# A gated graph network and graph attention on 128 graphs: the attention probabilities turned by one transposing DMA a group in place of four TensorE transposes, and the gather's second half in a bank of its own

## What is computed

```python
# layer 0: three rounds of message passing with a GRU cell
h = relu(layernorm(x))
for i in range(3):
    m = h @ weight[i]
    aggr = A^T @ m                    # A = (adj != 0), per graph
    h = gru_cell(aggr, h, w_ih, w_hh, b_ih, b_hh)
x = x + h
# layer 1: graph attention
h  = relu(layernorm(x))
Wh = h @ W.T
s1, s2 = Wh @ a1, Wh @ a2
e   = leaky_relu(s1[:, None] + s2[None, :], 0.2)
att = softmax(where(adj == 0, -inf, e))
x = x + att @ Wh
```

## Time and profile before

| | |
|---|---|
| time, median of 3 runs | 1867.82 us (1867.44 to 1868.47) |
| the profiled execution | 1866.37 us, of which 1864.6 us are its span |
| TensorE busy | 1797.0 us, 96% |
| VectorE, ScalarE, GpSimd busy | 1420.2 (76%), 1028.3 (55%), 346.5 (19%) us |
| granted TensorE clock, mean | 0.993 |
| DMA queue of the transfers | 26.7% of 16 engines |

### The profile page before, as it was taken

The page is one execution under the profiler, slowest core; times in us unless marked ns, Lnnn a source line. Parts: engine busy times, 40 slices in busy tenths (PEclk is TensorE's granted clock), DMA queues, the critical chain, the costliest instruction groups (busy, mean ns, idle before and its releaser), DMA issues.

```text
span 1864.6 us, 32405 instructions
## 1 busy us (share of the span) xinstructions
PE 1797.0 (96%) x10620; PEld 958.6 (51%) x10620; DVE 1420.2 (76%) x2801; ACT 1028.3 (55%) x1822; POOL 346.5 (19%) x778
## 2 busy tenths in 40 slices
PE   6999999999999999999999999999999999999995
PEld 5444555545555455555545555454554545555453
DVE  6667787777877877877777877777877777877776
ACT  5555555555555546555555556555555555555543
POOL 1022030311303122030310303113031220303101
PEclk9999999999999999999999999999999999999998
DMA  3323232322313223222222313223222322323111
GB/s 103 73 63 69 52 77 48 87 59 56 87 36 90 51 52 88 56 73 51 73 68 51 93 31 101 45 56 90 56 74 45 77 70 51 73 51 84 29 47 51
DMA packets 292000, 120.50 MB, mean 65 GB/s; under 512 B 207489, under 2 KB 291969, under 8 KB 291969
## 3 DMA queue, kind: packets, MB, share of 16 engines
q1 hardware_dynamic: 291968, 120.11, 26.7%
HBM read 52.96 MB, written 16.78 MB: 37 GB/s over the span
## 4 chain that ended last, share of the span: by engine, by line
issue 58%; POOL 13%; DVE 9%; PE 8%; ACT 7%; DMA 3%; POOLq 1%; ACTq 0%; DVEq 0%; SPq 0%
DMA ht_s<-h_s 3%; PE z_bank L318 3%; PE r_bank L318 2%; POOL ln_gnn L310 2%; DVE n_pre L887 2%; POOL ln_att L310 2%; ACT relu_gnn L270 2%; DVE dot_terms L933 1%; PE hn_bank L318 1%; ACT tanh_r L819 1%; PE in_bank L318 1%; ACT relu_att L270 1%; DVE stats_att L248 1%; ACT u_hi L845 1%; POOL ln_att L306 1%
## 5 line engine op out<-in xcount | busy, mean ns | idle before, releaser
L824 ACT ACTIVATE n_out<-n_pre,bih 128x512 f32<-128x512 f32 x192 | 137.9, 718 | 255.0 <-DVE n_pre L887 252.8
L318 PE MATMUL hn_bank<-ht_s,wh_hi 128*128 128x512 f16 x768 | 228.4, 379 | 1.7 <-PEq L426 1.7
L318 PE MATMUL r_bank<-ht_s,wh_hi 128*128 128x512 f16 x768 | 228.4, 379 | 0.0
L318 PE MATMUL z_bank<-ht_s,wh_hi 128*128 128x512 f16 x768 | 228.4, 379 | 0.0
L882 DVE SCALAR_TENSOR_TENSOR n_pre<-tanh_r,hn_b 128x512 f32<-128x512 f32 x192 | 146.2, 761 | 68.1 <-ACT tanh_r L819 65.1
L814 ACT ACTIVATE hn_b<-hn_bank,b_hn,down 128x512 f32<-128x512 f32 x192 | 147.5, 768 | 77.8 <-PE hn_bank L318 77.8
L819 ACT ACTIVATE tanh_r<-r_bank,b_rz,down 128x512 f32<-128x512 f32 x192 | 147.4, 768 | 68.9 <-PE r_bank L318 68.8
L833 ACT ACTIVATE ht_s<-ht 128x512 f16<-128x512 f32 x128 | 80.5, 629 | 186.7 <-DVE ht L903 186.7
L351 DVE TENSOR_TENSOR nb_lo<-nb_bank,nb_hi 128x512 f16<-128x512 f32 x192 | 131.2, 683 | 67.7 <-ACT nb_hi L347 67.6
L295 POOL TENSOR_TENSOR ln_gnn<-stats_gnn 128x4 f32<-128x4 f32 x32 | 12.9, 404 | 901.9 <-DVE stats_gnn L248 901.9
L828 ACT ACTIVATE tanh_z<-z_bank,b_rz,down 128x512 f32<-128x512 f32 x192 | 146.9, 765 | 35.9 <-PE z_bank L318 35.9
(11 more groups left out here) (180 smaller groups left out, 4053.2 us busy)
## 6 DMA issues: line engine op xcount, KB each, us to landing
x_in<-in_x_dram SPq DMA_DIRECT2D x32, 512.0 KB, 4.1
x_res<-in_x_dram SPq DMA_DIRECT2D x32, 512.0 KB, 4.1
out_dram<-x_out SPq DMA_DIRECT2D x32, 512.0 KB, 5.0
adj_in<-in_adj_dram SPq DMA_DIRECT2D x32, 256.0 KB, 4.2
adj_att<-in_adj_dram SPq DMA_DIRECT2D x32, 256.0 KB, 4.3
h_s<-ht_s SPq DMA_TRANSPOSE x128, 3.0
ht_s<-h_s SPq DMA_TRANSPOSE x64, 3.2
raw_ih<-in_L_gnn_w_ih_dram SPq DMA_DIRECT2D x2, 384.0 KB, 3.9
```

The source lines that it names most:

```text
L318: last = nc.tensor.matmul(bank_ap, w, d, start=start and i == 0, stop=stop and i == len(todo) - 1)
L824: nc.scalar.activation(n_out[c][:], n_pre[c][:], ACT.Tanh, bias=bih[:, 4 + c:5 + c]).then_inc(n_ready, 1)
```

## The change

The probabilities are split into high and low halves where they lie, with destination nodes on partitions, and both halves are turned at once by one DMA a group:

```diff
-                def probs_transpose(p, a):            # TensorE
-                    pe.wait_ge(prob_ready, per_group(p, a))
-                    for b in range(GROUP):
-                        last = nc.tensor.transpose(s_bank[:, b * P:(b + 1) * P], prob[:, b, :], ident[:])
-                    last.then_inc(probs_t_done, 1)
...
+                def probs_transpose(p, a):            # SP
+                    sp.wait_ge(prob_lo_ready, per_group(p, a))
+                    sp.sem_inc(sp_step, 1)
+                    wait_reached(sp, gather_done, per_chunk(p, a, 0) - 1)
+                    sp.sem_inc(sp_step, 1)
+                    sp.dma_start_transpose(pt_s[:].rearrange("p s b t -> p (s b) t"),
+                                           prob_s[:].rearrange("p s b t -> p (s b t)")).then_inc(pt_landed[a], 16)
...
-                def probs_transpose(p, a):            # ACT
-                    act.wait_ge(probs_t_done, per_group(p, a))
-                    wait_reached(act, gather_done, per_chunk(p, a, 0) - 1)
-                    nc.scalar.activation(pt_hi[:].rearrange("p b t -> p (b t)"), s_bank[:], ACT.Copy,
-                                         scale=PSCALE).then_inc(pt_hi_ready, 1)
+                def split_probs(p, a):
+                    act.wait_ge(prob_ready, per_group(p, a))
+                    if a == 1:
+                        act.wait_ge(pt_landed[0], per_load(p))
+                    else:
+                        wait_reached(act, pt_landed[1], per_load(p - 1))
+                    nc.scalar.activation(prob_s[:, 0], prob[:], ACT.Copy, scale=PSCALE).then_inc(prob_hi_ready, 1)
...
-                    dve.wait_ge(pt_hi_ready, n)
-                    nc.vector.scalar_tensor_tensor(pt_lo[:].rearrange("p b t -> p (b t)"), s_bank[:], PSCALE,
...
+                    dve.wait_ge(prob_hi_ready, n)
+                    nc.vector.scalar_tensor_tensor(prob_s[:, 1], prob[:], PSCALE, prob_s[:, 0], ALU.mult,
+                                                   ALU.subtract).then_inc(prob_lo_ready, 1)
```

The second half of the gather goes to `t_bank`, so that it no longer waits for the first half's reader; the residual that uses `t_bank` next waits for it instead:

```diff
         def gather_bank(p, half):
-            return r_bank if after_gates(p) and half == 1 else s_bank
+            if half == 0:
+                return s_bank
+            return r_bank if after_gates(p) else t_bank
...
                 def residual(p, a, c):
                     pe.wait_ge(h_ready, per_gate(p, a, LAYERS - 1, c))
                     wait_reached(pe, x1_ready, per_chunk(p, a, c) - 1)
+                    if a == 0 and c == 0:
+                        wait_reached(pe, vt_lo_ready, per_chunk(p - 1, 1, 1))
...
-                    pe.wait_ge(pt_lo_ready, per_group(p, a))
+                    pe.wait_ge(pt_landed[a], per_load(p))
...
+                    elif half == 1 and a == 0:
+                        pe.wait_ge(x1_ready, per_chunk(p, 1, 1))
                     elif half == 1:
-                        pe.wait_ge(vt_lo_ready, n - 1)
+                        pe.wait_ge(vt_lo_ready, n - 2)
+                    else:
+                        pe.wait_ge(sum_ready, per_group(p, a))
```

In the table, both gathers of group 1 move to `(5, 0)` and the residual of group 0 moves to `(5, 1)`:

```diff
-    (4, 7): [("gather", 1, 0, -1)],
-    (5, 0): [("residual", 0, 0, 0), ("update", 0, 2, 1, 0)],
-    (5, 1): [("gather", 1, 1, -1)],
+    (5, 0): [("gather", 1, 0, -1), ("gather", 1, 1, -1), ("update", 0, 2, 1, 0)],
+    (5, 1): [("residual", 0, 0, 0)],
```

More of the change, by code:

```diff
@@ L102 @@
     (5, 7): [("split_gnn", 1, 1), ("first_transpose", 1, 0, 1), ("first_transpose", 1, 1, 1), ("apply_att", 0, 0)],
+    (2, 6): [("split_probs", 0, -1), ("probs_transpose", 0, -1)],
 }
@@ L117 @@
 LAST_SLOT_SIDE = {
-    (5, 0): [("residual", 0, 0, 0), ("update", 0, 2, 1, 0)],
-    (5, 1): [("gather", 1, 1, -1), ("attend", 1, 0, -1)],
+    (5, 0): [("gather", 1, 0, -1), ("gather", 1, 1, -1), ("update", 0, 2, 1, 0)],
+    (5, 1): [("residual", 0, 0, 0), ("attend", 1, 0, -1)],
     (5, 2): [("residual", 0, 1, 0), ("stats_att", 0, 0)],
@@ L126 @@
         ("dots", 0, 1), ("scores", 0), ("apply_att", 1), ("split_att", 1), ("softmax", 0), ("dots", 1, 0),
-        ("dots", 1, 1), ("probs_transpose", 0), ("scores", 1), ("gather", 0, 0), ("gather", 0, 1),
-        ("softmax", 1), ("attend", 0, 0), ("probs_transpose", 1), ("attend", 0, 1), ("store", 0), ("gather", 1, 0),
+        ("dots", 1, 1), ("split_probs", 0), ("probs_transpose", 0), ("scores", 1), ("gather", 0, 0), ("gather", 0, 1),
+        ("softmax", 1), ("attend", 0, 0), ("split_probs", 1), ("probs_transpose", 1), ("attend", 0, 1), ("store", 0), ("gather", 1, 0),
         ("gather", 1, 1), ("attend", 1, 0), ("attend", 1, 1), ("store", 1)]
@@ L610, in graph_blocks @@
         prob = sb("prob", [P, GROUP, P], F32)
-        pt_hi = sb("pt_hi", [P, GROUP, P], F16)
-        pt_lo = sb("pt_lo", [P, GROUP, P], F16)
+        prob_s = sb("prob_s", [P, 2, GROUP, P], F16)
+        pt_s = sb("pt_s", [P, 2, GROUP, P], F16)
         row_max = sb("row_max", [P, GROUP], F32)
@@ L640, in graph_blocks @@
         res_t_done = sem("res_t_done")
-        gather_done, s2_done, probs_t_done, attend_done = (sem("gather_done"), sem("s2_done"), sem("probs_t_done"),
-                                                       sem("attend_done"))
+        gather_done, s2_done, attend_done = sem("gather_done"), sem("s2_done"), sem("attend_done")
+        pt_landed = [sem(f"pt_landed{a}") for a in range(2)]
         hn_ready, tanh_r_ready, n_ready, tanh_z_ready = (sem("hn_ready"), sem("tanh_r_ready"), sem("n_ready"),
@@ L652, in graph_blocks @@
         ht_lo_ready = sem("ht_lo_ready")
[L653 removed]
+        u_lo_ready, vt_lo_ready, prob_lo_ready = sem("u_lo_ready"), sem("vt_lo_ready"), sem("prob_lo_ready")
         dots_ready = sem("dots_ready")
@@ L784, in gather @@
                             last = products(target, [(u_hi[a][:, b, cols], u_lo[a][:, b, cols],
-                                                      pt_hi[:, b, :], pt_lo[:, b, :])])
+                                                      pt_s[:, 0, b, :], pt_s[:, 1, b, :])])
                     last.then_inc(gather_done, 1)
@@ L804, in _ @@
                     "residual": residual, "neighbours": lambda *which: neighbours_pe(pe, *which), "gather": gather,
-                    "scores": scores, "probs_transpose": probs_transpose, "attend": attend})
+                    "scores": scores, "attend": attend})
             @block.scalar
@@ L871, in _ @@
                     "gather": gather, "softmax": softmax,
-                    "probs_transpose": probs_transpose})
+                    "split_probs": split_probs})
             @block.vector
@@ L941, in scores @@
                     dve.wait_ge(adj_att_loaded[a], per_load(p))
-                    wait_reached(dve, probs_t_done, n - 1)
+                    wait_reached(dve, prob_lo_ready, n - 1)
                     nc.vector.tensor_scalar(prob[:], adj_att[a][:], 0.0, MASKED, ALU.is_equal,
@@ L959, in scores, with split_probs @@
                     nc.vector.tensor_scalar(minus_max[:], row_max[:], -1.0, None, ALU.mult).then_inc(minus_max_ready, 1)
-                def probs_transpose(p, a):
+                def split_probs(p, a):
                     n = per_group(p, a)
@@ L998, in _ @@
                     "neighbours": lambda *which: neighbours_dve(dve, *which), "gather": gather, "scores": scores,
-                    "probs_transpose": probs_transpose, "attend": attend})
+                    "split_probs": split_probs, "attend": attend})
             @block.gpsimd
```

12 lines of the change are left out of this document (4 added, 8 removed).

## The result

| | before | after |
|---|---|---|
| median of 4 runs, us | 1867.8 | 1952.9 (1952.4 to 1956.1) |
| ratio to before | | 1.0459, 95% interval 1.0441 to 1.0477 |
| span of the profiled execution, us | 1864.6 | 1951.3 |
| a pair in the loop, us | 112.66 | 117.1 to 119.1 |
| last `z` gate to the end, us | 36.5 | 42.9 |

A forecast was written before the change was run, and what follows sets the result against it. TensorE, busy 96% of the span, was taken as the bound, with new waits priced by ACT, DVE and POOL chains. 23.6 + 14.0 + 10 made 48 us, so 1916 us (2.6% slower), range 1878 to 1926.

The forecast's parts named there:

- The rival: PE's clock falls in each new wait, low for 6 us, 3 us lost 29 times, near 2000 us; chance 0.05.
- Taken off PE: Two times four transposes, 0.87 us a pair; with the waits of 0.44 and 1.57 us also gone, 2.9 us.
- Wait 1: At group 0's gather PE waits 2.45 us for the transposing DMA, making each pair 1.57 us longer.
- whatever PE does in between: From gate `r` of slot 5, step 5, to group 0's split lie 58.07 us, independent of PE's work.
- Wait 2: At the residual PE waits 2.3 us for the reader of the gather's second half; each pair 1.00 us longer.
- The pair without the clock: A loop pair goes from 112.66 us to 115.2 us, 2.57 us longer, with the clock staying at 1.00.
- The tail: After the gates, two DMA delays of 3.5 us each and 3 us for half clock: 10 us.
- The sum: Group 0's gathers 23.6 us, the second chain 14.0, tail 10: together 48 us longer, 1916 us on the median.
- the DMA in time: Landing 2 us sooner turns the loss at group 0's gather into some 0.4 us gain a pair; about 1882, chance 0.07.
- both chains giving way: ACT and DVE catch up with an earlier PE, so both chains start earlier; 1835 us, chance 0.08.
- nothing hid the residual's wait: Rival: only the residual's wait is hidden, for example by shorter POOL factors; about 1874 us, chance 0.05.
- What would show it: Trace signs: PE waits of 2.4 and 2.3 us, pair 115.2 us, split to gather 3.7 us, loop clock 1.00.

The follow-up runs named there:

- tail_pe: Changed kernel, but behind the last gate PE transposes the probabilities as before, and ACT and DVE split them out of `s_bank`; 1946.7 us.
- late3_tail: Changed kernel with group 0's gathers and slot 5's residuals and attends later, stats_gnn(1, 1) earlier, and PE's transposes behind the last gate; 1853.5 us.
- fill_both: Changed kernel plus unread matmuls in PE's two new waits of each loop pair, 9 before the `pt_s` wait, 13 before the residual's; 1916.1 us.
- bank_only: Kernel before with the bank part alone: gather's second half in `t_bank`, group 1's gathers and the residual reordered, no DMA; 1895.4 us.

## Why the prediction was wrong

**The step that failed** is in the rivals: "Two waits of 2.4 us a pair lie between 1.57 us (no fall in 14) and 3.09 us (none either), so I expect none." I read the absence of a fall behind two idle times as a rule for every idle time between them, and one of the two readings was itself wrong. The four transposes behind the idle time of 3.09 us took 0.63 us, at the upper level, but the clock fell right behind them. The trace of before has it (columns as in rows 3), and in tail_pe the clock is low already when the same transposes start:

```profile
1831.90:1832.60 0.70, 0.63 (x4) 0.42 (x4) 0.00 (x0) 0.00 (x0) 0.00 (x0) 1.00 0.00 0
1832.80:1837.60 4.80, 0.00 (x0) 0.00 (x0) 4.76 (x22) 0.00 (x0) 2.63 (x8) 0.50 0.00 0
```

```profile
1909.82 1.09 PE L765 MATMUL t_bank<-ident,ht 128*128 128x128 f32 x4 [3.08 <-DVE x_res L952]
```

PE had been idle again for 0.2 us at most when the clock fell, so the 5.05 us behind the transposes did not bring it down. All 14 kernels here have this wait of 3.1 us, and in all of them the clock falls between 0.9 us before its end and 1.7 us behind it. So the row that was taken as "none either" was a fall like those of the loop, and a wait of 3.1 us should have been priced as one. In the loop of after, waits of 2.2 us and of 3.0 to 3.2 were followed by the lower clock 24 times in 28. The rival had the mechanism, with 0.05, and with 3 us for each fall, by the nearest row of the tail; the measured loss is 1.7 us for each of 24. Its "near 2000" was 47 us off on the other side. The Trainium skill, page "TensorE: Matmul & The Clock Gate", in its section on the HAM clock gate, has activity keep the clock up and low as the default. The runs agree with that: unread matmuls in the waits held it at 1.00.

The other steps, in the forecast's order:

- **Taken off PE.** Right: 0.87 us a pair forecast, 0.7 measured in the loop of late3_tail.
- **Wait 1.** DVE's split to PE's gather was forecast at 3.68 us; the timelines of DVE, SP and PE have 1022.48, 1022.74 and 1025.84, so 3.36:

```profile
1021.80 0.68 DVE L982 SCALAR_TENSOR_TENSOR prob_s<-prob,prob_s 128x512 f16<-128x512 f32 x1
...
1022.74 1.24 SPq L711 DMA_TRANSPOSE pt_s<-prob_s  x1
```

  From DVE's end to SP's issue it is 0.26 us (0.25 in the earlier trace rows); from the issue to the consumer 3.10 us to PE here, 3.43 to POOL there. So the 3.68 did have slack: 0.25 and a landing of 3.1 make 3.35. From the start of the neighbours behind `r` of slot 5, step 5, to the gather lie 61.4 us in the changed kernel and in fill_both; forecast were 61.75 (924.98 to 986.73). So "whatever PE does in between" held, with slow stretches and without.
- **Wait 2.** From `x_out` of group 0 to the residual the forecast had 25.05 us, after has 25.55 (1044.23, in the line of DVE's timeline here, to 1069.78).

```profile
1044.23 0.88 DVE L999 SCALAR_TENSOR_TENSOR x_out<-w_bank,row_scale,x_res 128x256 f32<-128x256 f32 x2 [2.05 <-PE w_bank L318]
```

  The 0.5 is one instruction in this pair: POOL's power in the factors of stats_gnn.

```profile
1016.43 1.01 POOL L310 TENSOR_TENSOR ln_gnn<-ln_gnn,consts 128x4 f32<-128x4 f32 x1
```

```profile
1058.78 1.47 POOL L310 TENSOR_TENSOR ln_gnn<-ln_gnn,consts 128x4 f32<-128x4 f32 x1
```

```profile
1058.70 0.68 DVE L982 SCALAR_TENSOR_TENSOR prob_s<-prob,prob_s 128x512 f16<-128x512 f32 x1
```

  The first line is the timeline of POOL before, the second after, at the same place of a pair, and the third DVE's split, which starts 0.08 us ahead of the second. Before, the split has the same place (1016.35 in the earlier trace rows), but reads one input from PSUM (`pt_lo<-s_bank,pt_hi`); now both lie in SBUF. In before and bank_only the POOL instruction that starts within the split keeps its length in all 28 pairs (1.0 us for the power, 0.2 for the small ones). In the 12 kernels with the DMA part it is held up in all 168: 1.5 us for the power, or, where a small one is met instead, 0.5 to 0.7 for 0.2. So in some pairs of after, and in most of fill_both, a small one is longer and the power is not; there the chain is 25.7 to 25.8 us. "They cost nothing new" was said of the ACT copy and the DVE split with their source in SBUF; this is the cost. It is 0.4 to 0.8 us a pair, of which the shorter wait 1 gives back 0.3. The wait ahead of the gathers is 0.33 us, not 0.9. PE has done `r` 22.4 us behind `x_out` instead of 22.8, and the chain ends 0.5 us later; so the wait is 3.0 us instead of 2.3.
- **The pair without the clock.** 115.2 forecast, 115.4 to 115.7 in fill_both. The chains' term was right to 0.2 to 0.5 us, 3 to 7 us in all.
- **The tail.** 10 us forecast, 6.4 measured (36.5 to 42.9). Group 0's gather starts 3.15 us later behind the last `z` gate than before (3.5 forecast), and the end comes another 3.2 later. The second part was forecast at 6.5, 3.5 for the landing and 3 for the clock. Group 1's gather did run at the lower clock, but its 24 matmuls took 2.4 us where those of tail_pe took 1.3 at the upper level, a loss of 1.1. Group 0's gather ran at the lower clock in both kernels. What was too large is the 3 us for the clock.
- **The sum.** 48 forecast. Without the slow stretches 46 were measured (fill_both). That they agree to 2 us is partly luck: the pairs cost 3 to 7 us more than forecast, the tail 3.6 less. The excess of the result over the forecast, 37 us, is the term that had been set to zero.
- **The other rivals.** Neither the DMA in time (3.0 us at best again) nor both chains giving way occurred, and nothing hid the residual's wait. The landing time did turn out to depend on the size, 2.4 us at half of it.
- **What would show it.** I had said that "the clock stays at 1.00 in the loop". That was the line to read first, and only a stretch of a few us shows it; the page's row of 40 slices can't.
